# A two-layer transformer kernel on one core: GpSimd applies the layer norms that ScalarE applied, and does the multiply of the softmax normalisation that VectorE did

## The chip, the core and the metric

The kernel is one program on one core of a Trainium2 chip. The core has five instruction streams that matter here: TensorE (PE in the profile, with its weight loads as PEld), VectorE (DVE), ScalarE (ACT), GpSimd (POOL) and SyncE (SP), which issues the DMAs. They run at the same time and wait for one another through semaphores only. The metric is the time of one execution on the device in microseconds (us); lower is better.

## The reference

The input is 2 sequences of 1024 tokens with 128 features, in float32. Four sub-layers follow each other, and after each the result is added to its input and normalised:

```python
x = _layernorm(x + L0_attn(x))   # 16 heads of 8, causal
x = _layernorm(x + L0_ffn(x))    # 8 experts, the best 2 weighted, relu
x = _layernorm(x + L1_attn(x))   # low-rank q and k, 16 heads of 8, causal
x = _layernorm(x + L1_ffn(x))    # an attention of 16 heads of 4, not causal, then 8 experts, gelu

def _layernorm(x, axis=-1, eps=1e-05):
    m = jnp.mean(x, axis=axis, keepdims=True)
    v = jnp.var(x, axis=axis, keepdims=True)
    return (x - m) / jnp.sqrt(v + eps)

def attention(q, k, v):          # per head
    return softmax(scale * q @ k.T, axis=-1) @ v
```

So there are three attentions (two causal, one not) of 32 heads each (16 heads by 2 sequences), and two expert layers. The expert layers compute all 8 experts for all tokens and weight them by a gate.

## The kernel before

**Tiling.** The 2048 tokens are 16 tiles of 128 tokens (`NT`), in 4 chunks of 4 tiles (`NCH`, `TPC`); a sequence is 2 chunks. `x` and `x_plus` hold the tokens on the partitions, 128 features per tile; `xT` holds them turned round, as TensorE needs them.

**Attention.** The heads are numbered g = 0 to 95 and run one after another. Per head TensorE computes the scores twice. First by query (L1332), from which VectorE takes the largest score of each row (`find_max`: L1027 for full blocks, L1023 for blocks at the diagonal, which add the mask `future` first) and then the negated maximum of the head (L1033, `neg_max`). VectorE is two heads ahead (`AHEAD`). GpSimd splits the negated maximum into three bf16 parts (`split_max`, L719 to L726), TensorE turns them (L1354, `max_rows`), ScalarE copies them out (L888), and a DMA puts them among the rows of `qk`. Then TensorE computes the scores by key with the maximum already subtracted (L1346), ScalarE takes the exponential into `probs` (L911), GpSimd clears what lies beyond the diagonal in two chunks of each causal head (`mask`, L752), and TensorE multiplies by the values (L1375) and sums in one PSUM bank for a group of heads.

**Groups.** Heads are in groups of 3, 3, 3, 3, 2, 2 (causal) or 4, 4, 4, 4; that makes 12, 12 and 8 groups in the three attentions. When a group is complete, ScalarE copies the sums (L893), TensorE turns them (L1385), ScalarE copies them to `by_quarter` (L899), GpSimd adds them to `total` (`add_quarters`, L742 to L746, or L737), and VectorE normalises them (`normalise`): a reciprocal of the sum of each row (L1041) and a multiply of all results by it (L1043), which writes `a_tok`. VectorE does this two heads after the group's last head, between two of the head's parts.

**Between the heads.** Everything else (projections, statistics, norms, the next layer's q, k and v, the routing) is cut into steps, and tables filled by `put(...)` name the place at which each is done: `at_head(g, k)`, a part of a head, or `at_unit(f, m, half)`, a half of one of the 32 units (4 chunks by 8 experts) of an expert layer. Each engine goes through the same places in order and does its share of each step, in its function `between`. A step of a place inside the heads is done one place later (`at_place_before`).

**The layer norm** in those steps: VectorE computes mean and variance (`stats`, L1079 and L1082); GpSimd computes `rstd` = 1/sqrt(variance + eps) and `shift` = -mean * rstd (`root`, L676 to L679); ScalarE computes x = x_plus * rstd + shift for the 4 tiles of a chunk (`norm`, L853); TensorE turns the chunk (`xT`, L1422) and ScalarE copies that (L858). Norms are numbered k = 1 to 4, after each of the four sub-layers. The last chunk of k = 4 is VectorE's own (`last_units`), so ScalarE has 15 chunks of norms: 4 each for k = 1, 2, 3, and 3 for k = 4.

**Experts.** Unit by unit TensorE computes the hidden values (L1489), ScalarE applies relu or gelu (L931), TensorE multiplies back (L1501), and VectorE adds the result with its gate to `acc` (L1187). ScalarE does the activation of unit m+1 before the steps of unit m (`experts`, `hid(m + 1)` ahead of `between`).

## Time and profile before

| | us |
|---|---|
| median of 3 runs | 1165.69 (1164.51 to 1167.61) |
| the profiled execution | 1166.3 |
| its span, first to last instruction | 1164.6 |
| TensorE busy | 1077.7 (93%) |
| VectorE busy | 883.9 (76%) |
| ScalarE busy | 764.9 (66%) |
| GpSimd busy | 305.0 (26%) |

The busy times are averages over stages with different limits: the first causal attention runs from about 30 to 280 us, the first expert layer to about 410 us, the second causal attention to about 690 us, the attention without a mask to about 1037 us, and the second expert layer to the end. The mean granted clock of TensorE is 0.987 of full speed. In a list of groups or in a timeline, a row gives the start, the duration, the engine, the line and what is computed; what stands in brackets is how long the engine was idle just before and what ended that.

### The profile page before, as it was taken

The numbers are of one execution on the slowest core, as the hardware profiler recorded it, in microseconds if no ns is written. First come the engines' busy times: TensorE is split into PE (matmuls) and PEld (weight loads), VectorE is DVE, ScalarE is ACT, GpSimd is POOL, SyncE is SP. The second block draws the span as 40 slices with busy tenths as digits, with TensorE's granted clock in tenths as the row PEclk, the third lists the DMA queues.
The fourth block names the chain that finished last, engine by engine and source line by source line (L and its number), as shares of the span: only waits on it lengthen the run. The fifth ranks groups of instructions, "written<-read, shape, count | busy, mean of one in ns | idle before, by whom it ended". The sixth has DMA issues, their size and how long they took to land. (4 is left out here: it accounts for less than half of the span.)

```text
span 1164.6 us, 24392 instructions
## 1 busy us (share of the span) xinstructions
PE 1077.7 (93%) x8338; PEld 569.1 (49%) x8338; DVE 883.9 (76%) x2563; ACT 764.9 (66%) x1527; POOL 305.0 (26%) x843
## 2 busy tenths in 40 slices
PE   8999999989999988999999998898889898899997
PEld 5465665656767655666655532221122221137775
DVE  6999989882433497889978899799999899804435
ACT  4576776766444446777776677888888688875443
POOL 4234433231115225433346211230110100100001
PEclk9899999999999999999999999999999999999999
DMA  7355431100001601344222221002111000000000
GB/s 200 75 121 156 104 84 33 43 23 2 1 1 38 157 22 33 96 106 103 66 75 56 55 38 25 18 18 45 26 36 38 11 18 13 6 1 1 10 10 19
DMA packets 39563, 57.62 MB, mean 49 GB/s; under 512 B 9408, under 2 KB 14992, under 8 KB 39056
## 3 DMA queue, kind: packets, MB, share of 16 engines
q1 hardware_dynamic: 39440, 56.06, 19.6%
q8 instruction: 67, 1.10, 0.4%
q14 instruction: 56, 0.46, 0.1%
HBM read 30.81 MB, written 24.64 MB: 48 GB/s over the span
## 5 line engine op out<-in xcount | busy, mean ns | idle before, releaser
L911 ACT ACTIVATE probs<-bank 128x512 f32<-128x512 f32 x1088 | 575.9, 601 | 214.8 <-PE bank L1346 213.6
L1027 DVE TENSOR_REDUCE tile_max<-bank 128x1 f32<-128x512 f32 x768 | 495.5, 683 | 55.6 <-PE bank L1332 53.2
L1332 PE MATMUL bank<-qk 125*128 125x512 bf16 (+1 forms) x1280 | 387.2, 356 | 54.9 <-DVE tile_max L1027 41.3
L1346 PE MATMUL bank<-qk 128*128 128x128 bf16 (+1 forms) x1664 | 384.6, 309 | 5.9 <-ACT probs L911 5.5
L1375 PE MATMUL bank<-probs,v_head 128*32 128x512 f32 (+3 forms) x3328 | 304.1, 454 | 0.1
L1332 PEld LDWEIGHTS bank<-qk 125*128 125x128 bf16 (+1 forms) x1280 | 105.4, 96 | 333.1 <-DVE tile_max L1027 225.4
L1023 DVE CUSTOM_DVE_ANT_0 bank<-bank,future 128x512 f32<-128x512 f32 (+3 forms) x512 | 243.5, 506 | 22.2 <-PE bank L1332 22.1
L1187 DVE SCALAR_TENSOR_TENSOR acc<-bank,gate,acc 128x128 f32<-128x128 f32 x248 | 69.7, 343 | 158.4 <-PE bank L1501 158.4
L1346 PEld LDWEIGHTS bank<-qk 128*128 128x128 bf16 (+1 forms) x1664 | 138.2, 97 | 68.1 <-ACT probs L911 22.0
L1375 PEld LDWEIGHTS bank<-probs,v_head 128*32 128x32 f32 x3328 | 139.7, 109 | 53.4 <-issue 30.5
L931 ACT ACTIVATE probs<-bank,sb_b 128x512 f32<-128x512 f32 x128 | 81.0, 684 | 123.1 <-PE bank L1489 123.1
L1501 PEld LDWEIGHTS bank<-sb_w,probs 128*128 128x128 f32 x1024 | 123.2, 192 | 23.4 <-issue 22.5
L1501 PE MATMUL bank<-sb_w,probs 128*128 128x128 f32 x1024 | 125.0, 275 | 0.0
L1489 PE MATMUL bank<-xT,sb_w 128*128 128x512 f32 x256 | 121.0, 595 | 0.0
L752 POOL TENSOR_SCALAR_AFFINE_SELECT probs<-probs 128x512 f32<-128x512 f32 x128 | 81.5, 637 | 128.3 <-ACT probs L911 128.3
L719 POOL CAST neg_parts<-neg_max 128x8 bf16<-128x8 f32 x96 | 18.3, 191 | 298.1 <-DVE neg_max L1033 298.1
L1023 DVE DVE_READ_ACCUMULATOR2_ANT tile_max<- 128x1 f32 x512 | 71.9, 140 | 0.0
L1489 PEld LDWEIGHTS bank<-xT,sb_w 128*128 128x128 f32 x256 | 44.1, 191 | 34.0 <-issue 33.4
L742 POOL TENSOR_TENSOR pairs<-by_quarter 128x108 f32<-128x108 f32 (+1 forms) x24 | 9.5, 395 | 114.5 <-ACT by_quarter L899 114.5
L888 ACT ACTIVATE neg_rows<-bank 24x128 bf16<-24x128 bf16 x96 | 24.7, 257 | 15.0 <-PE bank L1354 15.0
L676 POOL TENSOR_SCALAR rstd<-mean_var 128x4 f32<-128x4 f32 (+1 forms) x11 | 2.6, 238 | 121.6 <-DVE mean_var L1082 121.4
L1354 PE MATMUL bank<-ident,neg_parts 128*24 128x128 bf16 x96 | 21.8, 227 | 7.5 <-POOL neg_parts L726 3.2
(148 smaller groups left out, 648.9 us busy)
## 6 DMA issues: line engine op xcount, KB each, us to landing
qk<-qk_parts SPq DMA_DIRECT2D x160, 144.0 KB
qk_parts<-q_parts SPq DMA_DIRECT2D x48, 192.0 KB, 2.4
qk_parts<-k_parts SPq DMA_DIRECT2D x48, 192.0 KB, 2.9
qk_parts<-q_parts SPq DMA_DIRECT2D x24, 96.0 KB, 2.3
qk_parts<-k_parts SPq DMA_DIRECT2D x24, 96.0 KB, 2.9
sb_w<-in_w SPq DMA_DIRECT2D x8, 256.0 KB, 3.7
sb_w<-in_w SPq DMA_DIRECT2D x2, 1024.0 KB, 5.9
qk<-neg_rows SPq DMA_DIRECT2D x96, 6.0 KB
```

The source lines that it names most:

```text
L752: nc.gpsimd.affine_select(out=p, in_=p, compare_op=ALU.is_ge, fill=0.0, base=0, pattern=[[0, 4], [1, P]], channel_multiplier=-1).then_inc( ...
L888: nc.scalar.activation(neg_rows[:, g % RING, :], neg_ps, ACT.Copy).then_inc(sem("neg_rows"), 1)
L911: nc.scalar.activation(probs[:, hd.probs_place(c), :], S2[i % len(S2)][:], ACT.Exp, scale=hd.a.scale).then_inc(sem("probs"), 1)
L931: nc.scalar.activation(hidden[:, m % 2, fb, :], hid_bank(f, m, fb)[:], ACT.Relu if f == 0 else ACT.Gelu, bias=w_sb[f"b1_{f}"][:, FB * e + ...
L1023: ins = nc.vector.tensor_tensor_reduce(out=s1[:, at:at + P * count], in0=s1[:, at:at + P * count], in1=future[:, P * (4 - count):4 * P], s ...
L1027: ins = nc.vector.tensor_reduce(largest, s1[:, at:at + P * count], AX.X, ALU.max)
L1187: ins = nc.vector.scalar_tensor_tensor(acc[:, tile, :], y_bank(f, m)[:, P * t:P * (t + 1)], gate[:, tile, e:e + 1], acc[:, tile, :], ALU.m ...
L1332: ins = mm(s1[:, at:at + P * count], qk[hd.query_rows, hd.place, 0, P * t:P * (t + 1)], qk[hd.query_rows, hd.place, 1, P * k0:P * (k0 + co ...
L1346: ins = mm(s2[:, at:at + P * count], qk[hd.key_rows, hd.place, 1, P * j:P * (j + 1)], qk[hd.key_rows, hd.place, 0, P * q0:P * (q0 + count) ...
L1375: ins = mm(SUM[Q * quarter:Q * (quarter + 1), q:q + P * count], v_head_of(a)[:, hd.v_slot, j, :], probs[:, hd.probs_place(c), at:at + P * ...
L1489: ins = mm(hid_bank(f, m, fb)[:], w_sb[f"w1_{f}"][:, e, P * fb:P * (fb + 1)], xT[:, tokens(c)], start=True, stop=True)
L1501: ins = mm(y[:, P * t:P * (t + 1)], hidden[:, m % 2, fb, P * t:P * (t + 1)], w_sb[f"w2_{f}"][:, e, fb, :], start=fb == 0, stop=fb == FB - 1)
```

## The change

GpSimd takes over two pieces of work. First, all norms with k < 4 (12 chunks of 4 instructions) move from ScalarE (`activation`) to GpSimd (`tensor_scalar` with a multiply and an add). GpSimd does them in the same table's places. Second, `normalise` is split: VectorE keeps the reciprocal (now `inverse`), and GpSimd does the multiply, 32 instructions, in part k = 1 of the head in which VectorE did it, after its own mask of that part. The semaphores are renamed to fit, and VectorE gets a wait ahead of the reciprocal for the multiply of two groups earlier.

```diff
+def by_gpsimd(k, c):
+    return k < 4
...
+        def normed(eng, k, c):
+            by = by_gpsimd(k, c)
+            eng.wait_ge(sem("normed_gpsimd" if by else "normed"), NORMS_OF[by].index((k, c)) + 1)
... GpSimd, between(place)
+                    if kind == "norm" and by_gpsimd(*which):
+                        k, c = which
+                        pool.wait_ge(sem("rstd"), ROOT_OF[(k, c)])
+                        for t in range(TPC * c, TPC * (c + 1)):
+                            ins = nc.gpsimd.tensor_scalar(x[:, t, :], x_plus[:, t, :], rstd[:, t:t + 1], shift[:, t:t + 1],
+                                                          ALU.mult, ALU.add)
+                        ins.then_inc(sem("normed_gpsimd"), 1)
... GpSimd, add_quarters(i)
-                ge(pool, "normalised", 2 * (i - 1))
+                ge(pool, "normalised", i - 1)
... GpSimd
+            def normalise(i):
+                first = GROUPS[i][0]
+                a, G, h = first.a, len(GROUPS[i]), first.h
+                o = total[:, i % 2, :, 0:G * a.dv].rearrange("p t (g d) -> p t g d", g=G)
+                pool.wait_ge(sem("inverse"), i + 1)
+                nc.gpsimd.tensor_tensor(
+                    a_tok[:, of_sequence(first.b), a.hd * h:a.hd * (h + G)].rearrange("p t (g d) -> p t g d", g=G),
+                    o[:, :, :, 1:a.dv], den_inv[:, i % 2, :, 0:G].unsqueeze(3).to_broadcast([P, TB, G, a.hd]),
+                    ALU.mult).then_inc(sem("normalised"), 1)
... GpSimd, head(run, g)
                     if k == 1 and hd.a.causal:
                         mask(g, 1)
+                    if k == 1 and g - 2 >= run.start and HEADS[g - 2].ends_group:
+                        normalise(GROUP[g - 2])
... GpSimd, after the last head of a run
                 add_quarters(GROUP[run.stop - 1])
+                normalise(GROUP[run.stop - 1])
... ScalarE, between(place)
-                    if kind == "norm":
+                    if kind == "norm" and not by_gpsimd(*which):
... VectorE (normalise, now inverse)
                 dve.wait_ge(sem("total"), ADDS[i + 1])
-                nc.vector.reciprocal(den_inv[:, i % 2, :, 0:G], o[:, :, :, 0]).then_inc(sem("normalised"), 1)
-                dve.wait_ge(sem("normalised"), 2 * i + 1)
-                nc.vector.tensor_tensor(
-                    a_tok[:, of_sequence(first.b), a.hd * h:a.hd * (h + G)].rearrange("p t (g d) -> p t g d", g=G),
-                    o[:, :, :, 1:a.dv], den_inv[:, i % 2, :, 0:G].unsqueeze(3).to_broadcast([P, TB, G, a.hd]),
-                    ALU.mult).then_inc(sem("normalised"), 1)
+                ge(dve, "normalised", i - 1)
+                nc.vector.reciprocal(den_inv[:, i % 2, :, 0:G], o[:, :, :, 0]).then_inc(sem("inverse"), 1)
... TensorE, step aT
-                        pe.wait_ge(sem("normalised"), 2 * groups_done)
+                        pe.wait_ge(sem("normalised"), groups_done)
... TensorE, step xT (the store of the output and the step bias wait in the same way)
-                        pe.wait_ge(sem("normed"), NORM_OF[(k, c)])
+                        normed(pe, k, c)
```

The order of VectorE's instructions around the first group's normalisation (head 4 of the first attention), before and then now. `ISA` is the masked maximum (L1023), `TENSOR_REDUCE` the plain one (L1027); in the changed kernel they have the lines 1053 and 1057.

```order
L1027 TENSOR_REDUCE tile_max<-bank 128x1 [waits scores_q]
L1023 ISA bank,tile_max<-bank,future 128x384 [waits scores_q]
L1023 ISA tile_max 128x1
L1023 ISA bank,tile_max<-bank,future 128x128
L1023 ISA tile_max 128x1
L1041 RECIPROCAL den_inv<-total 128x8x3 [waits total]
L1043 TENSOR_TENSOR a_tok<-total,den_inv 128x8x24 [waits normalised]
L1027 TENSOR_REDUCE tile_max<-bank 128x1 [waits scores_q]
L1023 ISA bank,tile_max<-bank,future 128x256 [waits scores_q]
```

Now:

```order
L1057 TENSOR_REDUCE tile_max<-bank 128x1 [waits scores_q]
L1053 ISA bank,tile_max<-bank,future 128x384 [waits scores_q]
L1053 ISA tile_max 128x1
L1053 ISA bank,tile_max<-bank,future 128x128
L1053 ISA tile_max 128x1
L1072 RECIPROCAL den_inv<-total 128x8x3 [waits total]
L1057 TENSOR_REDUCE tile_max<-bank 128x1 [waits scores_q]
L1053 ISA bank,tile_max<-bank,future 128x256 [waits scores_q]
```

The multiply and its wait for the reciprocal have gone from between the maxima; nothing else moved.

GpSimd's instructions in the same head 4, before. The two `AFFINE_SELECT` are the masks, `COPY` is the values of head 6, and the four after the second mask split the maximum of head 6.

```order
L752 AFFINE_SELECT probs<-probs 128x512 [waits probs]
L711 COPY v_head<-v 128x8x9 [waits pv]
L752 AFFINE_SELECT probs<-probs 128x512 [waits probs]
L719 CAST neg_parts<-neg_max 128x8 [waits neg_max,neg_ps]
L721 TENSOR_TENSOR neg_rest<-neg_max,neg_parts 128x8 [waits neg_parts]
L724 CAST neg_parts<-neg_rest 128x8 [waits neg_parts]
L726 TENSOR_TENSOR neg_parts<-neg_rest,neg_parts 128x8 [waits neg_parts]
```

Now:

```order
L779 AFFINE_SELECT probs<-probs 128x512 [waits probs]
L728 COPY v_head<-v 128x8x9 [waits pv]
L779 AFFINE_SELECT probs<-probs 128x512 [waits probs]
L770 TENSOR_TENSOR a_tok<-total,den_inv 128x8x24 [waits inverse]
L736 CAST neg_parts<-neg_max 128x8 [waits neg_max,neg_ps]
L738 TENSOR_TENSOR neg_rest<-neg_max,neg_parts 128x8 [waits neg_parts]
L741 CAST neg_parts<-neg_rest 128x8 [waits neg_parts]
L743 TENSOR_TENSOR neg_parts<-neg_rest,neg_parts 128x8 [waits neg_parts]
```

The multiply stands between the second mask and the split, with a wait for VectorE's reciprocal.

GpSimd's instructions in the first expert layer, from the root of the norm after the attention on, before:

```order
L676 TENSOR_SCALAR rstd<-mean_var 128x8 [waits var]
L677 TENSOR_TENSOR rstd<-rstd,minus_half 128x8 [waits gpsimd_chain]
L678 TENSOR_TENSOR shift<-mean_var,rstd 128x8 [waits gpsimd_chain]
L679 TENSOR_SCALAR shift<-shift 128x8 [waits gpsimd_chain]
L698 TENSOR_TENSOR pick<-pick,small 128x64 [waits route_weights]
L698 TENSOR_TENSOR pick<-pick,small 128x64 [waits gpsimd_chain]
L699 TENSOR_TENSOR gate<-pick 128x64 [waits gpsimd_chain]
```

Now:

```order
L686 TENSOR_SCALAR rstd<-mean_var 128x8 [waits var]
L687 TENSOR_TENSOR rstd<-rstd,minus_half 128x8 [waits gpsimd_chain]
L688 TENSOR_TENSOR shift<-mean_var,rstd 128x8 [waits gpsimd_chain]
L689 TENSOR_SCALAR shift<-shift 128x8 [waits gpsimd_chain]
L695 TENSOR_SCALAR x<-x_plus,rstd,shift 128x128 [waits rstd]
L695 TENSOR_SCALAR x<-x_plus,rstd,shift 128x128 x3
L695 TENSOR_SCALAR x<-x_plus,rstd,shift 128x128 [waits rstd]
L695 TENSOR_SCALAR x<-x_plus,rstd,shift 128x128 x3
L715 TENSOR_TENSOR pick<-pick,small 128x64 [waits route_weights]
L715 TENSOR_TENSOR pick<-pick,small 128x64 [waits gpsimd_chain]
L716 TENSOR_TENSOR gate<-pick 128x64 [waits gpsimd_chain]
```

The eight instructions of the two chunks follow the root directly on GpSimd; in the kernel before they stood on ScalarE, among its activations.

## Rows read from the trace of the kernel before

**Rows 1.** The page, busy time of each engine, its share of the span, and instructions.
```profile
PE 1077.7 (93%) x8338; PEld 569.1 (49%) x8338; DVE 883.9 (76%) x2563; ACT 764.9 (66%) x1527; POOL 305.0 (26%) x843
```

**Rows 2.** Busy us by stretch: PE, PEld, DVE, ACT, POOL; then TensorE's clock, DMA.
```profile
30.00:280.00 250.00, 237.68 (x2250) 143.42 (x2250) 209.66 (x729) 172.04 (x360) 89.01 (x266) 0.98 0.29 75
282.00:410.00 128.00, 123.10 (x713) 89.39 (x712) 52.30 (x219) 54.69 (x99) 33.22 (x50) 1.00 0.20 45
...
815.00:915.00 100.00, 89.02 (x649) 22.74 (x645) 95.47 (x167) 83.00 (x168) 10.33 (x49) 1.00 0.16 31
```

**Rows 3.** TensorE's waits, 30 to 380 us: for whom, us in total, times, longest.
```profile
PE bank L1332 <- DVE tile_max L1023: 4.6, 18, 0.6
...
PE bank L1332 <- DVE tile_max L1027: 3.1, 6, 0.7
```

**Rows 4.** The same, 700 to 1000 us.
```profile
PE bank L1332 <- DVE tile_max L1027: 31.8, 88, 3.7
```

**Rows 5.** Timeline, head 4: VectorE's normalisation, and TensorE after it.
```profile
67.79 0.30 DVE L1041 RECIPROCAL den_inv<-total 128x24 f32<-128x24 f32 x1
68.13 0.36 DVE L1043 TENSOR_TENSOR a_tok<-total,den_inv 128x192 f32<-128x192 f32 x1
68.40 0.68 DVE L1027 TENSOR_REDUCE tile_max<-bank 128x1 f32<-128x512 f32 x1
...
70.01 0.38 PE L1332 MATMUL bank<-qk 125*128 125x512 bf16 x1 [0.26 <-DVE tile_max L1023]
```

**Rows 6.** Timeline, head 7: GpSimd, VectorE and TensorE.
```profile
88.89 1.28 POOL L666 TENSOR_TENSOR x_plus<-x,sb_bo 128x512 f32<-128x512 f32 x1
...
89.35 1.03 DVE L1043 TENSOR_TENSOR a_tok<-total,den_inv 128x192 f32<-128x192 f32 x1
...
91.04 0.39 PE L1332 MATMUL bank<-qk 125*128 125x128 bf16 x2 [0.54 <-DVE tile_max L1027]
```

**Rows 7.** Timeline, third attention: the multiply and what follows it on VectorE.
```profile
831.50 0.29 DVE L1043 TENSOR_TENSOR a_tok<-total,den_inv 128x128 f32<-128x128 f32 x1
831.71 1.88 DVE L1027 TENSOR_REDUCE tile_max<-bank 128x1 f32<-128x512 f32 x3
```

**Rows 8.** Timeline, first expert layer: root, ScalarE's norms, TensorE's transposes.
```profile
304.21 0.26 POOL L679 TENSOR_SCALAR shift<-shift 128x8 f32<-128x8 f32 x1
...
304.92 1.64 ACT L853 ACTIVATE x<-x_plus,shift,rstd 128x128 f32<-128x128 f32 x4
...
306.61 0.66 PE L1422 MATMUL bank<-ident,x 128*128 128x128 f32 x4 [1.10 <-ACT x L853]
...
309.49 0.66 PE L1422 MATMUL bank<-ident,x 128*128 128x128 f32 x4 [0.50 <-ACT x L853]
```

**Rows 9.** Timeline, same layer, the norm after the experts, first chunk.
```profile
339.56 0.25 POOL L679 TENSOR_SCALAR shift<-shift 128x4 f32<-128x4 f32 x1
...
342.77 0.66 PE L1422 MATMUL bank<-ident,x 128*128 128x128 f32 x4 [1.10 <-ACT x L853]
```

**Rows 10.** GpSimd's groups by form: busy us and mean ns of one, then idle.
```profile
L677 POOL TENSOR_TENSOR rstd<-rstd,minus_half 128x8 f32<-128x8 f32 x4 | 6.7, 1676 | 0.3
...
L742 POOL TENSOR_TENSOR pairs<-by_quarter 128x108 f32<-128x108 f32 x16 | 6.7, 419 | 73.3 <-ACT by_quarter L899 73.3
...
L627 POOL TENSOR_SCALAR_AFFINE_SELECT ident<-ident 128x128 f32<-128x128 f32 x1 | 0.3, 294 | 0.2 <-POOL ident L625 0.2
```

**Rows 11.** GpSimd's timeline in head 4: the second mask, then the split.
```profile
69.54 0.64 POOL L752 TENSOR_SCALAR_AFFINE_SELECT probs<-probs 128x512 f32<-128x512 f32 x1 [1.83 <-ACT probs L911]
71.53 0.19 POOL L719 CAST neg_parts<-neg_max 128x8 bf16<-128x8 f32 x1 [1.35 <-DVE neg_max L1033]
```

**Rows 12.** TensorE's timeline after a ScalarE norm: head 22, then head 68.
```profile
204.09 0.39 PE L1346 MATMUL bank<-qk 128*128 128x384 bf16 x2 [0.47 <-ACT probs L911]
...
730.54 0.39 PE L1346 MATMUL bank<-qk 64*128 64x512 bf16 x1 [0.74 <-ACT probs L911]
...
739.35 0.66 PE L1422 MATMUL bank<-ident,x 128*128 128x128 f32 x4 [0.98 <-ACT x L853]
```

More of the change, by code:

```diff
@@ L326 @@
 ROOT_OF = {(step[1], c): i + 1 for i, step in enumerate(ROOTS) for c in step[2]}
-NORM_OF = {step[1:]: i + 1 for i, step in enumerate(NORMS)}
 STATS = [step for place in PLACES for step in BETWEEN[place] if step[0] == "stats"]
@@ L330 @@
 assert all(len([step for step in BETWEEN[place] if step in TAKEN]) <= 1 for place in PLACES)
+def by_gpsimd(k, c):
+    return k < 4
+NORMS_OF = {by: [step[1:] for step in NORMS if by_gpsimd(*step[1:]) == by] for by in (False, True)}
 THIRDS = [step for place in PLACES for step in BETWEEN[place] if step[0] == "split"]
@@ L602, in _ @@
             for c in range(NCH - 1):
-                sp.wait_ge(sem("normed"), NORM_OF[(4, c)])
+                normed(sp, 4, c)
                 store_out(tiles(c))
@@ L664, in between @@
                             loaded(pool, "attn1")
-                            pool.wait_ge(sem("normed"), NORM_OF[(2, c)])
+                            normed(pool, 2, c)
                         nc.gpsimd.tensor_tensor(x_plus[:, tiles(c), :], x[:, tiles(c), :],
@@ L1034, in find_max, with inverse @@
                                             negate=True).then_inc(sem("neg_max"), 1)
-            def normalise(i):
+            def inverse(i):
                 first = GROUPS[i][0]
-                a, G, h = first.a, len(GROUPS[i]), first.h
+                a, G = first.a, len(GROUPS[i])
                 o = total[:, i % 2, :, 0:G * a.dv].rearrange("p t (g d) -> p t g d", g=G)
                 dve.wait_ge(sem("total"), ADDS[i + 1])
-                nc.vector.reciprocal(den_inv[:, i % 2, :, 0:G], o[:, :, :, 0]).then_inc(sem("normalised"), 1)
-                dve.wait_ge(sem("normalised"), 2 * i + 1)
-                nc.vector.tensor_tensor(
-                    a_tok[:, of_sequence(first.b), a.hd * h:a.hd * (h + G)].rearrange("p t (g d) -> p t g d", g=G),
-                    o[:, :, :, 1:a.dv], den_inv[:, i % 2, :, 0:G].unsqueeze(3).to_broadcast([P, TB, G, a.hd]),
-                    ALU.mult).then_inc(sem("normalised"), 1)
+                ge(dve, "normalised", i - 1)
+                nc.vector.reciprocal(den_inv[:, i % 2, :, 0:G], o[:, :, :, 0]).then_inc(sem("inverse"), 1)
             def head(run, g, found):
@@ L1059, in head @@
                     if k == 0 and g - 2 >= run.start and HEADS[g - 2].ends_group:
-                        normalise(GROUP[g - 2])
+                        inverse(GROUP[g - 2])
                 return found
@@ L1191, in experts @@
                     if m == 0:
-                        normalise(last)
+                        inverse(last)
                     between(at_unit(f, m, 1))
```

## The prediction

> **What bounds the kernel now.** I read the page's busy times first [rows 1]. TensorE is busy 93% of the span, GpSimd 26%. The change takes work from VectorE (76%) and ScalarE (66%), so it can gain only where TensorE waits for one of them, or where one of them sets the pace. Busy time by stretch shows where that is [rows 2]. In the first causal attention TensorE is busy 237.7 of 250 us; in the experts 123.1 of 128 us, with VectorE and ScalarE under half busy; in a steady piece of the attention without mask VectorE is busy 95.5 of 100 us and TensorE 89.0. So the first 690 us and the last 120 us go by TensorE plus its waits, and the stretch between goes by VectorE. TensorE's waits by releaser come next: up to 380 us it waits 4.6 + 3.1 = 7.7 us for VectorE's maxima [rows 3], from 700 to 1000 us 31.8 us [rows 4]. Last I read the timeline around each instruction that moves, to see whether one of these waits hangs on it.
>
> **The multiply in the causal attentions (24 of the 32).** It takes VectorE 0.27 us from start to start (68.13 to 68.40), and the reciprocal ahead of it takes 0.34 us because the multiply waits for it [rows 5]; without that wait it should be some 0.07 us less. So about 0.34 us leave VectorE each time. Behind 17 of the 24 multiplies, within 3.5 us, TensorE waits for a maximum that came late, as in [rows 5] at 70.01: 0.26 us. Head by head these waits are 0.26 us in 7 cases, 0.17 or 0.18 us in 5, over 0.34 us in 5. I credit the smaller of wait and 0.34 us: 7 x 0.26 + 5 x 0.174 + 4 x 0.34 = 4.05. The fifth of the last kind is the multiply of 1.03 us beside GpSimd's bias add, 0.96 us from start to start, behind which TensorE waits 0.54 and once more 0.26 us [rows 6]: 0.80. Together 4.85 us. Seven multiplies have no such wait behind them and give nothing. If each freed wait turned up at the next instruction the term would be 0; if the whole 24 x 0.34 came back it would be 8.2. I take 4.8.
>
> **The multiply in the third attention.** Here VectorE sets the pace, so what leaves it leaves the span: 0.21 us from start to start (831.50 to 831.71) [rows 7] and 0.07 for the wait, 0.28 us. Five multiplies lie in the steady part (831 to 1009 us): 1.4 us. Three more (694, 744, 790 us) lie where next-layer projections also load TensorE; all eight would give 2.2. I take 1.4.
>
> **What the multiply costs on GpSimd.** The trace has no such instruction. Two inputs of 108 elements take 0.42 us, of 512 elements 1.28 us, that is 2.1 ns an element [rows 6, 10], so 192 elements take about 0.60 and 128 about 0.46 us: 17 us in all, on an engine with 860 us free. In head 4 VectorE's reciprocal ends at 68.09, GpSimd leaves its second mask at 70.18 and then stands idle 1.35 us until the maximum of head 6 arrives [rows 5, 11]. The multiply fits in that gap, so the split behind it starts when it did. Queued behind it are that split and the next head's mask, for which TensorE waits; only a multiply of more than the gap's 1.35 us would begin to move them. In the third attention the wait for the reciprocal ends three quarters of a head before the split is due. Cost 0.
>
> **The norms in the first expert layer (k = 1 and 2, five chunks).** GpSimd has `shift` at 304.47, but ScalarE first ends the activations of the next unit and starts at 304.92; its four instructions end at 306.56, and TensorE waited 1.10 us, from 305.51. The second chunk costs it 0.50 us more [rows 8]. The chunk of the next norm: `shift` ready at 339.81, TensorE there at 341.67, and again a wait of 1.10 us [rows 9]; two more chunks repeat this (361.15, 397.05, again 1.10 us each, arriving 1.55 and 1.80 us after `shift`). On GpSimd the four follow the root at once. One of them is 128 elements with one tensor input: the nearest row is the select of 128x128, 0.29 us; at the two-input rate it would be 0.46 us; the dearest row per element is the power, 1.68 us for 8 [rows 10], a different algorithm, which I keep as a rival. I take 0.38 us from start to start, 1.55 us for a chunk. Then the first chunk is ready at 306.1 (gain 0.45), the second before TensorE is (0.50), the others at 341.4 (1.10), 0.05 us late (1.05) and in time (1.10): 4.2 us. At 0.46 us an instruction this is 3.5, at 0.29 us 4.7.
>
> GPSIMD Engine Reference of the Trainium skill, § Engine selection, speaks against both moves in one way: it sends elementwise work to VectorE, two-input work being about twice as slow on GpSimd, and calls one-input work roughly line-rate. By it the norms are the cheap half and the multiplies the dear one, which the rows on GpSimd bear out (0.29 against 0.46 us for 128 elements).
>
> **The norms elsewhere.** In the causal attentions TensorE turns the chunk later than GpSimd would have it. The gain is that ScalarE is not held for 1.6 us: 0.47 us behind the norm of head 22 [rows 12], and 0.33 and 0.31 us at 212.1 and 590.0, where TensorE waited for ScalarE's queue: 1.1 us (0 to 1.6). In the third attention the two norms cost TensorE waits of 0.74, 0.70 and 0.98 us (the first and third of them in [rows 12]), 2.4 us; VectorE sets the pace of this attention on the whole, so I let half of it through: 1.2 (0 to 2.4).
>
> **Sum.** 4.8 + 1.4 + 4.2 + 1.1 + 1.2 = 12.7 us. The profiled execution took 1166.3 us (span 1164.6 and 1.7 around it), 0.6 above the median of the runs, so the span should become 1151.9, its execution 1153.6, and the median 1165.7 - 12.7 = **1153.0 us**.
>
> **Rivals.** *Only the norms pay* (1159.2 us): the multiplies' 6.2 us do not come, because TensorE's next limit stands right behind each wait, or because GpSimd's new reads hold up VectorE. For it: TensorE has no time to spare in the causal stretch [rows 2]. Against it: the waits are measured and stand directly behind the multiply. The port is told by [rows 6]: a multiply with two SBUF inputs took 1.03 us, ending just after GpSimd's read, against 0.36 alone [rows 5]. Perfetto Trace Analysis of the Trainium skill, § Optimizing Scalar/DVE Operations, warns that moving work between these two might not help because they share a port; SBUF — State Buffer, § Who interferes with whom, limits this to VectorE instructions with two SBUF inputs or in a two-port mode. By the first page the sum would be 6.5; by the second the multiplies moved are just the ones that collide, and the maxima, with at most one input in SBUF, are safe. The trace has only [rows 6] on this, and agrees.
>
> *Next to nothing* (1163 us): in addition GpSimd's norm instruction costs nearer 0.6 us, so that the first chunk in the experts comes later than ScalarE's and the other three hardly earlier (gain 1.5 us), with 1.1 from ScalarE. The waits of 0.17 to 0.26 us are then model noise.
>
> *Slower* (1190 us): GpSimd's `tensor_scalar` with two operands per partition runs on a slow path. It decides from about 1.1 us an instruction, where the five expert chunks wait 8.5 us longer, as much as the other terms give. At 2 us a chunk takes 8 us: in the experts TensorE waits 5.9, 4.6, 5.1, 5.3 and 5.1 us longer (26), some 2 us at head 22 and 4 where masks and splits are held behind a norm, less 7 for the multiplies: 25 us slower. For it: the power at over 150 ns an element. Against it: the select, a one-input instruction of the same size, at 0.29 us.
>
> **How the numbers follow.** 0.3% (3.5 us) is about what a measurement of this kernel can tell from no change. Forecast 0.62, only the norms 0.18, next to nothing 0.13, slower 0.07. Faster is the first two, 0.80; same 0.13; slower 0.07. The range goes from all upper ends (8.2, 2.2, 4.7, 1.6 and 2.4: 19.1 us, 1147), less a little because all together are unlikely, so 1148, up to just short of the third case, 1162; that leaves out the slower one and most of the third.
>
> **What would show it.** In the new profile: about 0.26 us waits gone behind the 24 reciprocals of the causal attentions; no VectorE instruction of 1.03 us there; TensorE's waits ahead of its transposes of `x` (up to 1.10 us before) down to one or two; the GpSimd norm at 0.3 to 0.45 us an instruction; heads of the third attention at a group's end 0.28 us shorter; GpSimd busy some 35 us more (17 for multiplies, 18 for norms), ScalarE 23 us less. I am wrong if a norm instruction takes over 0.6 us, if TensorE waits for the split maxima in more than the one place it did, or if the maxima themselves grow longer.

## The result, and the profile after

The changed kernel takes 1148.8 us (median of 4 runs, 1146.31 to 1150.53), the kernel before 1165.35 us (4 runs, 1164.51 to 1167.61). The ratio is 0.9853 with a 95% interval of 0.983 to 0.9876: 17.1 us less, and between 14.4 and 19.8. The forecast was 1153.0 us, 12.7 us less. The direction was right and the size was short: 12.7 us where 17.1 were measured. The time lies inside the stated range of 1148 to 1162 us, at its lower edge. The rest of this document looks for the missing 4.4 us.

The profiled execution after took 1146.3 us, its span 1144.6, against 1164.6 before: 20.0 us less. It is the fastest of its four runs, so not all of those 20 us belong to the change.

The page's busy times after, which answer to [rows 1]:

```profile
PE 1067.2 (93%) x8273; PEld 569.3 (50%) x8338; DVE 872.2 (76%) x2531; ACT 745.2 (65%) x1479; POOL 338.2 (30%) x923
```

VectorE has the 32 multiplies less, ScalarE the 48 instructions of the norms, and GpSimd has both (80 more instructions, 33.2 us more). The stretches of [rows 2] (columns as there): the first over the same 250 us, the other two at the places where the same work now lies.

```profile
30.00:280.00 250.00, 238.88 (x2240) 147.28 (x2273) 204.63 (x715) 171.92 (x357) 98.01 (x288) 0.98 0.28 75
277.00:401.00 124.00, 122.83 (x713) 89.36 (x712) 51.80 (x218) 47.22 (x79) 42.22 (x71) 1.00 0.20 46
785.00:885.00 100.00, 88.99 (x647) 20.99 (x643) 97.19 (x167) 84.09 (x171) 10.98 (x53) 1.00 0.19 36
```

The expert stretch holds the same 713 TensorE matmuls in 124 us instead of 128. TensorE's waits up to 380 us (for whom, us in total, times, longest), which answer to [rows 3]:

```profile
PE bank L1358 <- DVE tile_max L1053: 3.6, 12, 0.6
...
PE bank L1358 <- DVE tile_max L1057: 1.1, 3, 0.5
PE bank L1448 <- POOL x L695: 1.1, 2, 0.9
```

The waits for maxima fell from 7.7 to 4.7 us. From 700 to 1000 us, though, they did not fall at all against [rows 4] (31.8 us in 88):

```profile
PE bank L1358 <- DVE tile_max L1057: 32.1, 91, 3.7
```

In that attention TensorE waits for VectorE all along, 91 times in 300 us. What a saving is worth there can't be read from the sum of the waits, only from how far apart the heads lie.

Head 4 shows the exchange, first on VectorE, then on GpSimd, then on TensorE (they answer to [rows 5] and [rows 11]):

```profile
67.60 0.30 DVE L1072 RECIPROCAL den_inv<-total 128x24 f32<-128x24 f32 x1
67.81 0.63 DVE L1057 TENSOR_REDUCE tile_max<-bank 128x1 f32<-128x512 f32 x1
```

```profile
69.35 0.63 POOL L779 TENSOR_SCALAR_AFFINE_SELECT probs<-probs 128x512 f32<-128x512 f32 x1 [1.84 <-ACT probs L941]
69.95 0.52 POOL L770 TENSOR_TENSOR a_tok<-total,den_inv 128x192 f32<-128x192 f32 x1
71.00 0.19 POOL L736 CAST neg_parts<-neg_max 128x8 bf16<-128x8 f32 x1 [0.53 <-DVE neg_max L1063]
```

```profile
69.48 0.38 PE L1358 MATMUL bank<-qk 125*128 125x512 bf16 x1
```

From the reciprocal to the next maximum VectorE now needs 0.21 us instead of 0.61. The multiply fills GpSimd's gap, and the split behind it still waits for VectorE. TensorE's wait of 0.26 us is gone.

**The ledger.** In every head TensorE turns the split maxima once (L1354 before, L1380 after): 96 markers, which are the same instruction in every variant. I compare their starts between two traces. A step is what the distance of two neighbouring markers shrank by; it bears the number of the later one. At most heads it repeats to 0.02 us from kernel to kernel. The exceptions are heads 1, 2 and 12 (head 12 takes 6.89 to 7.80 us in the thirteen traces, whatever the kernel) and the heads in which TensorE's granted clock was at half for a stretch. Around head 9, before and after:

```profile
88.44 0.23 PE L1354 MATMUL bank<-ident,neg_parts 128*24 128x128 bf16 x1
...
96.26 0.23 PE L1354 MATMUL bank<-ident,neg_parts 128*24 128x128 bf16 x1
```

```profile
87.91 0.23 PE L1380 MATMUL bank<-ident,neg_parts 128*24 128x128 bf16 x1
...
94.73 0.23 PE L1380 MATMUL bank<-ident,neg_parts 128*24 128x128 bf16 x1
```

96.26 - 88.44 = 7.82 us before and 94.73 - 87.91 = 6.82 after: a step of 1.00 us, behind the multiply that took 1.03 us [rows 6]. All steps, sorted by cause (the experiments below bear the sorting out), against the forecast:

| term | forecast, us | steps found | us |
|---|---|---|---|
| multiply, causal attentions | 4.8 | 15 heads, 0.21 to 0.46 each, once 1.00 | 5.6 |
| multiply, third attention | 1.4 | 9 heads, 0.37 to 0.39 each | 3.4 |
| norms, first expert layer | 4.2 | one, over the whole layer | 3.9 |
| norms, causal attentions | 1.1 | 0.80, 0.75, 0.79 | 2.3 |
| norms, third attention | 1.2 | 2.58 within the 4.16 of head 70 | 2.6 |
| sum | 12.7 | | 17.8 |
| TensorE's clock, heads 70 and 88 | - | 1.58 within the same 4.16, and 0.31 | 1.9 |
| head 12, no cause assigned | - | 0.17 | 0.2 |

With 0.2 us at the start this accounts for the 20.0 us between the two spans, to 0.1 us. The causes give 17.8, within the interval of the ratio.

Head 88, from marker 87 to marker 88, holds neither a multiply nor a norm. TensorE's clock is the last column but two (0.50 is the lower of its two levels, 1.2 GHz, 1.00 the upper, 2.4 GHz). Before, then after:

```profile
926.60:933.40 6.80, 6.62 (x27) 1.18 (x31) 5.17 (x11) 3.72 (x8) 1.80 (x8) 0.50 0.00 1
```

```profile
907.40:914.20 6.80, 5.98 (x26) 0.98 (x29) 5.18 (x11) 3.09 (x6) 1.79 (x8) 0.50 0.00 0
```

Marker 87 stands at 932.72 before and at 914.15 after, so before head 88 has 0.7 us of the half clock in it and after none. It takes 10.51 us before and 10.21 after. In the other traces it takes 10.20 or 10.21 us where the stretch is over by its start, and 10.63, 10.83 and 11.11 where 0.9, 1.3 and 1.9 us of it reach in (the experiments below with the norms alone, the split root and two norms).

### The profile page after: what moved, and what is told of

It is laid out like the page before. It is cut to its first block and busy times, and to the rows that moved or that the text cites. A ratio compares the mean times of both kernels' runs of the same rounds, so it can differ in the third digit from the quotient of the medians.

```text
span 1144.6 us, 24357 instructions
## 1 busy us (share of the span) xinstructions
PE 1067.2 (93%) x8273; PEld 569.3 (50%) x8338; DVE 872.2 (76%) x2531; ACT 745.2 (65%) x1479; POOL 338.2 (30%) x923
## 3 DMA queue, kind: packets, MB, share of 16 engines
q1 hardware_dynamic: 39440, 56.06, 19.8%
## 5 line engine op out<-in xcount | busy, mean ns | idle before, releaser
L1372 PE MATMUL bank<-qk 128*128 128x128 bf16 (+4 forms) x1599 | 360.0, 306 | 3.9 <-ACT probs L941 3.6
L1372 PEld LDWEIGHTS bank<-qk 128*128 128x128 bf16 (+1 forms) x1664 | 138.6, 97 | 64.0 <-ACT probs L941 17.6
L1380 PE MATMUL bank<-ident,neg_parts 128*24 128x128 bf16 x96 | 21.8, 227 | 7.3 <-POOL neg_parts L743 3.2
```

Of the source, the lines that this page charges most:

```text
L1372: ins = mm(s2[:, at:at + P * count], qk[hd.key_rows, hd.place, 1, P * j:P * (j + 1)], qk[hd.key_rows, hd.place, 0, P * q0:P * (q0 + count) ...
```

## The experiments

**The multiply alone.** The changed kernel with all norms back on ScalarE:

```diff
 def by_gpsimd(k, c):
-    return k < 4
+    return False
```

> The changed kernel with all norms back on ScalarE: only the multiply is on GpSimd. Theory (the two halves are independent, each returns the waits that hang on it): the step between the traces at the group ends of the causal attentions is 5.8 us in all and of the third attention 3.7 us, so 9.5 us less than before, 1156 us, with no change in the expert layers. Rival 'only the norms pay' from the prediction: within 2 us of before. Rival 'overlap' (the norms had freed the same waits already): clearly more than 9.5 us, 12 or above.

**The norms alone.** The kernel before, in which VectorE keeps the multiply, with the norms of the change:

```diff
+def by_gpsimd(k, c):
+    return k < 4
... GpSimd, between(place)
+                    if kind == "norm" and by_gpsimd(*which):
... ScalarE, between(place)
-                    if kind == "norm":
+                    if kind == "norm" and not by_gpsimd(*which):
```

> The kernel before with only the 12 norm chunks moved to GpSimd; VectorE keeps its multiply. Theory (independent halves): 3.9 us in the first expert layer, 2.3 in the causal attentions and 4.2 in the third attention, 10.4 us in all, 1155 us. The prediction's own terms for this half: 6.5 us, 1159 us. Overlap: the sum of the two halves is then well off 20 us of the profiled executions.

On that chip the kernel before took 1166.07 us (16 runs). The multiply alone: 1156.82 us (1153.3 to 1157.65), ratio 0.9913 [0.9891, 0.9935], 10.1 us less. The norms alone: 1157.2 us (1153.79 to 1157.98), ratio 0.9905 [0.9878, 0.9932], 11.1 us less. By the ledger they are 5.6 + 3.4 = 9.0 and 3.9 + 2.3 + 2.6 = 8.8 us. Both halves pay and they add up within their intervals (10.1, from 7.6 to 12.7, and 11.1, from 7.9 to 14.2). *Only the norms pay* forecast nothing from the multiplies, and falls. The steps of the multiply in the table stand in the first of these traces with the same values, to 0.01 us, save head 87, where the half-clock stretch is 3.4 us long and not 6.8; they are missing in the second. For the norms it is the other way round (0.95 us and not 0.79 at head 55). That is what sorts the table. Head 12, which I had counted with the multiply in the 5.8 that I expected, shrinks by 0.38 us with the norms alone too, and the 3.7 had head 88 in it. The 4.2 us that I expected of the third attention's norms were the whole step of head 70, clock included.

**Two chunks of norms alone.** The kernel before, with only the two norms of the third attention on GpSimd:

```diff
+def by_gpsimd(k, c):
+    return k == 3 and c >= 2
```

> The kernel before with only two norm chunks moved (k = 3, the two chunks of the second sequence, which fall into the third attention). Theory: there ScalarE is loaded so highly that a norm of 1.6 us between two exponentials stops TensorE and then VectorE, and nothing catches up: 4.2 us less, 1161 us. Rival (the prediction's term, VectorE sets the pace and hides half): 1.2 us less.

1163.55 us over 10 runs, against 1166.07 over 16 runs of the kernel before on that chip; ratio 0.9973 [0.9961, 0.9986], so 3.1 us (1.6 to 4.5) by the ratio and 2.5 by the medians. That excludes the 1.2 of the prediction's term, but not my 4.2. The step at head 70 is again 4.16 us, of which the ledger gives 2.58 to the norms, a little more than TensorE's three waits of 0.74, 0.70 and 0.98 us [rows 12]. So all of the waits came back, not the half I let through. In this trace TensorE turns both chunks without waiting, here the first:

```profile
733.56 0.66 PE L1439 MATMUL bank<-ident,x 128*128 128x128 f32 x4
```

With the norms on ScalarE the three waits stand as before (the trace of the multiply alone):

```profile
722.74 0.39 PE L1372 MATMUL bank<-qk 64*128 64x512 bf16 x1 [0.73 <-ACT probs L941]
723.83 0.39 PE L1372 MATMUL bank<-qk 64*128 64x512 bf16 x1 [0.70 <-ACT probs L941]
729.97 0.66 PE L1448 MATMUL bank<-ident,x 128*128 128x128 f32 x4 [0.98 <-ACT x L883]
```

VectorE's rows of the same place say why they count in full. First the multiply alone, then the changed kernel:

```profile
726.15 2.49 DVE L1057 TENSOR_REDUCE tile_max<-bank 128x1 f32<-128x512 f32 x4 [2.08 <-PE bank L1358]
...
730.99 0.69 DVE L1057 TENSOR_REDUCE tile_max<-bank 128x1 f32<-128x512 f32 x1 [0.89 <-PE bank L1358]
```

```profile
720.09 2.48 DVE L1057 TENSOR_REDUCE tile_max<-bank 128x1 f32<-128x512 f32 x4 [0.71 <-PE bank L1358]
722.75 1.89 DVE L1057 TENSOR_REDUCE tile_max<-bank 128x1 f32<-128x512 f32 x3 [0.17 <-PE bank L1358]
```

VectorE itself stood idle here, waiting for TensorE, and for less time once the norms had left ScalarE. It does not set the pace in this part of the attention, whatever its busy share is on the whole.

**The multiply without its stall.** The kernel before; VectorE keeps the multiply but does one maximum between the reciprocal and it.

```diff
                 nc.vector.reciprocal(den_inv[:, i % 2, :, 0:G], o[:, :, :, 0]).then_inc(sem("normalised"), 1)
+            def multiply(i):
...
                 dve.wait_ge(sem("normalised"), 2 * i + 1)
... head
                         for i in range(found, upto):
                             find_max(i)
+                            if left:
+                                multiply(left.pop())
...
                         normalise(GROUP[g - 2])
+                        left.append(GROUP[g - 2])
...
```

> The kernel before, all work on its old engine, but VectorE does one maximum between the reciprocal and the multiply that waits for it. That takes away the stall (0.34 to 0.22 us from start to start in the causal attentions, 0.38 to 0.26 in the third) and no work. Theory (every bit of VectorE's time at these places counts): 0.12 us at each of 8 places of the third attention and at 17 causal ones, 3.0 us less in the profiled execution. Rival (the stall is hidden, only the multiply's own time counts): no change.

1162.91 us (7 runs), ratio 0.9964 [0.9948, 0.998]: 4.2 us less (2.3 to 6.1). VectorE's rows in head 4, where the spacing from reciprocal to maximum was 0.34 us ahead of the multiply [rows 5] and is now 0.22:

```profile
69.87 0.30 DVE L1041 RECIPROCAL den_inv<-total 128x24 f32<-128x24 f32 x1
70.09 0.63 DVE L1027 TENSOR_REDUCE tile_max<-bank 128x1 f32<-128x512 f32 x1
70.63 0.34 DVE L1048 TENSOR_TENSOR a_tok<-total,den_inv 128x192 f32<-128x192 f32 x1
70.89 0.42 DVE L1023 CUSTOM_DVE_ANT_0 bank<-bank,future 128x256 f32<-128x256 f32 x1
```

So the same work without the wait gives 0.18 or 0.19 us back at 21 groups' ends, in all three attentions, and 0.60 at head 9, where the multiply meets less of the bias add (it took 0.60 us). Of the 0.19, 0.12 is the wait; the rest is that the maximum behind the reciprocal takes 0.63 us and not 0.68. The prediction had put the wait at 0.07 us, which was too low. Where the prediction had found no late maximum for TensorE behind a causal group's multiply, the whole change returned nothing, as it had said.

**The collision at 89 us.** The kernel before, with the second bias add placed one head earlier:

```diff
-for c, g in enumerate((4, 6, 8, 10)):
+for c, g in enumerate((4, 5, 8, 10)):
```

> The kernel before with one GpSimd instruction moved: the bias add of the second chunk (128x512, 1.28 us) stands a head earlier, so that it no longer overlaps VectorE's multiply of head 7, which took 1.03 us beside it. Theory (the multiply was held by GpSimd's read): it takes 0.36 us like the others, and TensorE reaches the turn of the maxima of head 9 about 0.66 us earlier, measured from head 6 (the step of 1.00 us of the changed kernel there, less the 0.34 us of an ordinary group). Rival (the 1.03 us had another cause, a wait for something else in head 7): it stays at 1.03 us, no step.

One run: 1166.99 us, where the kernel before ran between 1164.64 and 1168.8 on that chip, so the total tells nothing. The rows do. The multiply that took 1.03 us [rows 6]:

```profile
89.17 0.36 DVE L1043 TENSOR_TENSOR a_tok<-total,den_inv 128x192 f32<-128x192 f32 x1
89.45 0.68 DVE L1027 TENSOR_REDUCE tile_max<-bank 128x1 f32<-128x512 f32 x1
```

0.36 us instead of 1.03, with GpSimd idle beside it, and a step of 0.67 us at head 9. The same was seen at two more places: beside a GpSimd instruction with two inputs the multiply took 0.65 us at 607.3 before, and 1.16 us at 459.9 in the kernel without the stall. The rule of the Trainium skill weighed in the prediction (SBUF — State Buffer, § Who interferes with whom) holds in this case. The maxima, which by that page are safe, did not lengthen beside GpSimd's new work either: after, 24 whole ones that overlap a multiply or a norm there took 0.68 us each at the median, and so did the 471 with GpSimd idle.

**How much slack a norm on GpSimd has.** The changed kernel; each norm instruction is done twice, once into a tile that nobody reads (ahead of it, cut here, stand that tile and a wait for the norm of the same chunk before):

```diff
...
-                            ins = nc.gpsimd.tensor_scalar(x[:, t, :], x_plus[:, t, :], rstd[:, t:t + 1], shift[:, t:t + 1],
-                                                          ALU.mult, ALU.add)
+                            for into in (spare, x):
+                                ins = nc.gpsimd.tensor_scalar(into[:, t, :], x_plus[:, t, :], rstd[:, t:t + 1],
+                                                              shift[:, t:t + 1], ALU.mult, ALU.add)
```

> The changed kernel with each of GpSimd's 48 norm instructions done twice (once into a spare tile), so a chunk takes 3.4 us in place of 1.7. Theory (GpSimd has room everywhere but in the first expert layer, where TensorE waits for the norm directly): TensorE's waits ahead of its transposes of x grow by 1.5, 0.9, 1.5, 1.8 and 1.6 us in the expert layer, 7.3 us in all, and under 1 us is added in the attentions. Rival (GpSimd's order matters in the attentions too: masks and split maxima are held up): 2 us or more are added between the turns of the maxima of heads 22 to 25, 53 to 55 and 67 to 70.

One run: 1163.9 us, span 1162.2, so 17.6 us longer than after. TensorE's waits from 280 to 412 us, in this kernel and in the changed one:

```profile
PE bank L1452 <- POOL x L699: 8.0, 4, 2.6
```

```profile
PE bank L1448 <- POOL x L695: 1.1, 2, 0.9
```

The waits in the expert layer grew by 6.9 us, as expected (7.3), though the layer grew by 10.2. In this trace it holds two stretches of half clock, from 306.9 and 364.9 us, which the trace after has not; they begin 0.4 and 1.3 us behind waits of 2.58 and 1.96 us, so they may well be part of the price. In the attentions I had expected under 1 us and found 5.4, at heads 25, 35, 55 and 70. That is the amount of the rival (2 us or more), by another path. Beside each stands a wait of TensorE of 0.7 to 1.8 us ahead of a transpose of `x`, the longest here:

```profile
595.39 0.66 PE L1452 MATMUL bank<-ident,x 128*128 128x128 f32 x4 [1.79 <-POOL x L699]
```

So the norms in the attentions have less slack on GpSimd than one chunk's time, 1.74 us, and in these heads no wait of TensorE for a mask or a split was added.

**The last layer's norms too.** The changed kernel with three more chunks on GpSimd:

```diff
-    return k < 4
+    return True
```

> The changed kernel with the three norm chunks of k = 4 on GpSimd as well. In the second expert layer nothing turns the result, only the store waits for it, and ScalarE is under half busy. Theory (a norm costs only where TensorE waits for it or for ScalarE behind it): the same as the changed kernel, within 0.5 us. Rival (ScalarE's 1.6 us delay the next activation there): 1 to 3 us less.

1148.13 us (4 runs, 1146.3 to 1151.98), ratio 0.9839 [0.981, 0.9869]: the same as the changed kernel.

**Is the third attention VectorE's?** The prediction said that it sets the pace there. If so, work moved off its way, or added to it, must show in every head. The changed kernel with `neg_max` taken only behind the next head's first maximum:

```diff
                 ins.then_inc(sem("max_taken"), 1)
+                take_neg_max()
                 if c == a.chunks - 1:
...
-                    nc.vector.tensor_reduce(neg_max[:, hd.slot, :], tile_max[:, hd.slot], AX.X, ALU.max,
-                                            negate=True).then_inc(sem("neg_max"), 1)
+                    ready.append(g)
...
```

> The changed kernel, with one more stall taken from VectorE: the negated maximum of a head is computed after the first maximum of the next head instead of directly behind the last maximum that it waits for. That saves about 0.11 us a head and moves no work to another engine. Theory (in the third attention VectorE sets the pace, all of what leaves it comes back; in the causal ones only where TensorE waits): 0.11 us at each of some 30 heads, 3.3 us less than the changed kernel in the third attention, and 1 to 3 us in the causal ones; 1144 us. Rival (the maximum then comes 0.5 us later to GpSimd, and TensorE, which took its split 0.4 to 0.6 us after it was ready, waits for it): no gain or a loss.

1149.4 us (1146.62 to 1151.44), ratio 0.9852 [0.9831, 0.9873]: no gain, which is the rival's outcome. The expected 3.3 us did not come; from the marker of head 64 to that of head 95 the trace is 0.95 us longer than after. Six heads in which a group is normalised are 0.08 to 0.11 us shorter, twelve others, from 66 to 94, are 0.09 to 0.10 longer, and head 84 is 0.35 longer. Then the reverse: the changed kernel with a `memset` of 128x128 on VectorE in each of the 32 heads, once in the middle of the head, once right behind `neg_max`.

```diff
+                if not a.causal and c == 2:
+                    nc.vector.memset(extra[:, g % 16, :], 0.0)
```

```diff
                     nc.vector.tensor_reduce(neg_max[:, hd.slot, :], tile_max[:, hd.slot], AX.X, ALU.max,
                                             negate=True).then_inc(sem("neg_max"), 1)
+                    if not a.causal:
+                        nc.vector.memset(extra[:, g % 16, :], 0.0)
```

> The changed kernel with one idle VectorE instruction added per head of the third attention (a memset of 128x128 in a spare tile, 32 in all), behind the third maximum of the head, where VectorE runs without waiting. New theory (VectorE sets the pace inside a head, TensorE at the change of heads, where VectorE waits about 0.18 us for the first scores): the memset's start-to-start time, estimated at 0.1 to 0.2 us from VectorE's other short instructions, comes on top of the span 32 times: 3 to 6 us between the turns of the maxima of heads 63 and 95. Old theory (VectorE sets the pace throughout): the same.

> The same memset, but directly behind the negated maximum of each head, at the change of heads. New theory: it fills the time in which VectorE waits for TensorE's scores there, so less than 1 us is added in the same stretch. Old theory (VectorE sets the pace throughout): the same 3 to 6 us as with the memset inside the head.

One run each: 1151.01 and 1148.67 us, which by themselves tell nothing at this size. The instruction costs VectorE 0.08 us from start to start:

```profile
822.06 0.17 DVE L1067 MEMSET extra<- 128x128 f32 x1
822.14 1.32 DVE L1058 TENSOR_REDUCE tile_max<-bank 128x1 f32<-128x512 f32 x2
```

If VectorE set the pace everywhere, 32 times 0.08 us = 2.6 us would show. In the middle it shows as 0.08 or 0.09 us at seven heads (71, 75, 79, 83, 87, 91, 95) and as nothing in the others; these seven are where a group ends and the reciprocal stands. That is 0.6 us, so both theories, with their 3 to 6 us, were wrong there. Behind `neg_max` it shows at eleven other heads (66, 68, 74, 76, 78, 80, 82, 86, 90, 92, 94), 0.9 us in all, as expected. Head 88 has a half-clock stretch in it and tells nothing. So whether VectorE's time counts depends on the place within the head: in its middle it counts only in the one head in four that has the normalisation, at its end in about one of three, and at the other places VectorE has at least 0.08 us to spare. What sets the pace there I have not found.

**An earlier start in the experts.** The changed kernel, the last norms on GpSimd too, and a root for each chunk, the first of them one place earlier:

```diff
-    put(at[4], ("stats", k, c1))
-    put(at[5], ("root", k, (c0, c1)))
+    put(at[4], ("stats", k, c1), ("root", k, (c0,)))
+    put(at[5], ("root", k, (c1,)))
...
-    return k < 4
+    return True
```

> The changed kernel with all norms but the last chunk's on GpSimd, and the root of the two chunks after an attention computed chunk by chunk, the first one place earlier. In the first expert layer the changed kernel's TensorE still waits 0.85 us for the first chunk's norm, behind a power of 1.68 us for 8 columns; with 4 columns the power takes 1.04 us, so the chunk is ready some 0.6 us earlier. Theory: the step in the first expert layer is 0.6 us, nothing elsewhere; the time cannot be told from the changed kernel's. Rival (the additional 2 us of GpSimd's work hold up masks and split maxima in the attentions): 0.5 us or more is lost at heads 21 to 24 and 52 to 55.

1149.85 us (4 runs, 1149.0 to 1150.76), ratio 0.986 [0.9839, 0.9881]: no gain, and the first expert layer is 0.14 us longer, not 0.6 shorter. The second chunk's root now stands in GpSimd's queue ahead of the first chunk's norm and costs what the split saved. GpSimd, then TensorE:

```profile
300.16 0.24 POOL L689 TENSOR_SCALAR shift<-shift 128x4 f32<-128x4 f32 x1
300.48 0.23 POOL L686 TENSOR_SCALAR rstd<-mean_var 128x4 f32<-128x4 f32 x1
300.79 1.05 POOL L687 TENSOR_TENSOR rstd<-rstd,minus_half 128x4 f32<-128x4 f32 x1
...
302.43 2.62 POOL L695 TENSOR_SCALAR x<-x_plus,rstd,shift 128x128 f32<-128x128 f32 x6
```

```profile
304.23 0.66 PE L1448 MATMUL bank<-ident,x 128*128 128x128 f32 x4 [0.95 <-POOL x L695]
```

None of the variants is clearly faster than the changed kernel.

## Why the prediction came out as it did

**The multiply, causal attentions: 4.8 forecast, 5.6 measured.** The mechanism was right and the term too small. I had credited the smaller of TensorE's wait and 0.34 us. The seven heads with waits of 0.26 us returned 0.33, four of the five with 0.17 or 0.18 returned 0.22 and the fifth nothing, and three with more returned 0.45. What left VectorE ahead of the next maximum was 0.39 us (0.61 to 0.22), since the wait for its own reciprocal costs 0.12 us and not 0.07. The collision was as read: 1.00 us at head 9 (forecast 0.80), of which 0.67 is shown by moving the bias add.

**The multiply, third attention: 1.4 forecast, 3.4 measured; the largest error.** Two factors. From the reciprocal to the second maximum behind it VectorE took 1.19 us before and 0.81 after, so 0.38 us left it and not 0.28; and it came back at eight groups' ends, not at five. Those where projections also load TensorE, which I had left out, paid like the rest. A ninth step, 0.37 us at head 90, is in every trace with the multiply on GpSimd and in no other; that head has no multiply, and why it gained is open. The reason that I gave, that what leaves VectorE leaves the span there, held for the heads with the normalisation. It is no rule for the others, as the moved `neg_max` and the two added instructions show: there it depends on the place.

**The multiply on GpSimd: 0 forecast, 0 found.** One took 519 ns for 192 elements (0.60 expected), and nothing was held up. GpSimd's own waits for the reciprocal, 17.3 us in all, show in no wait of another engine, and TensorE waits for the split maxima once, 3.2 us, as before:

```profile
L770 POOL TENSOR_TENSOR a_tok<-total,den_inv 128x192 f32<-128x192 f32 (+1 forms) x32 | 14.9, 466 | 17.3 <-DVE den_inv L1072 17.3
```

**The norms in the experts: 4.2 forecast, 3.9 measured.** The price of one instruction was set between 0.29 and 0.46 us at 0.38; it is 448 ns long and 0.43 from start to start, a chunk 1.74 us:

```profile
L695 POOL TENSOR_SCALAR x<-x_plus,rstd,shift 128x128 f32<-128x128 f32 x48 | 20.8, 448 | 0.4
```

At the two-input end, 0.46 us, the forecast was 3.5. TensorE's two later arrivals, which I gave as 1.55 and 1.80 us behind `shift`, are 1.65 and 1.87 us in the trace before; that changes the sum by 0.05 us. The first chunk still makes TensorE wait 0.85 us (1.10 before [rows 8]), and the chunk of [rows 9] is in time:

```profile
299.32 0.26 POOL L689 TENSOR_SCALAR shift<-shift 128x8 f32<-128x8 f32 x1
...
301.47 0.66 PE L1448 MATMUL bank<-ident,x 128*128 128x128 f32 x4 [0.85 <-POOL x L695]
...
333.77 0.24 POOL L689 TENSOR_SCALAR shift<-shift 128x4 f32<-128x4 f32 x1
334.12 1.74 POOL L695 TENSOR_SCALAR x<-x_plus,rstd,shift 128x128 f32<-128x128 f32 x4
...
335.92 0.66 PE L1448 MATMUL bank<-ident,x 128*128 128x128 f32 x4
```

The price is one and a half times the select's, so what the prediction drew from the Trainium skill (GPSIMD Engine Reference, § Engine selection), that one-input work is the cheap kind on GpSimd, did not hold here: one norm lasts 0.45 us and a two-input multiply of 128 elements 0.41 us.

**The norms, causal: 1.1 forecast, 2.3 measured.** The three places were the right ones, but each gave 0.75 to 0.80 us where I had credited 0.31 to 0.47, the wait shown. The failed step is this cap: the 1.6 us that left ScalarE were worth more than the one wait that carried ScalarE's name. Where the rest of each lay I have not traced.

**The norms, third attention: 1.2 forecast, 2.6 measured.** Halving them for the attention's overall bound was the failed step. The waits fell where VectorE itself waited for TensorE.

**What no term of the sum had: the clock.** The trace before holds, in the same head 70, a stretch in which TensorE's granted clock was at half. Just ahead of it TensorE was busy 5.71 of 7.90 us and had two waits for ScalarE's exponentials, of 0.74 and 0.70 us. Before it and in it, the columns as in [rows 2]:

```profile
724.00:731.90 7.90, 5.71 (x41) 1.26 (x37) 7.71 (x14) 7.06 (x16) 0.94 (x5) 1.00 0.00 1
732.00:735.40 3.40, 3.40 (x17) 0.99 (x16) 0.00 (x0) 1.46 (x4) 0.54 (x1) 0.50 0.56 108
```

and the same work with the multiply alone, whose clock did not fall behind the same two waits:

```profile
716.00:733.00 17.00, 13.84 (x99) 3.85 (x95) 13.46 (x24) 15.26 (x34) 2.23 (x11) 1.00 0.11 22
```

Without the stretch the step between before and the multiply alone is still 1.58 us at this head, where neither a multiply nor a norm differs; VectorE's idle time there fell from 3.63 to 2.08 us. I read that as the stretch's price. The same difference stands at head 38, which takes 8.34 us before with such a stretch and 6.82 in the multiply alone without. Whether the 1.6 us belong to chance or to the change is open. Of the four traces in which ScalarE does these two norms, three have a half-clock stretch at head 70 (before, the stall taken away, the bias add apart); of the nine in which GpSimd does them, none has. That speaks for a share of the norms' move in it, and no run tests it by itself. In the timed runs the whole change is worth 17.1 us, with either reading inside its interval.

**The rivals.** *Next to nothing* rested on a norm instruction near 0.6 us and on waits that were model noise: the instruction took 0.43, and the waits came back more than whole. *Slower* needed 1.1 us. Doubling the instruction, to some 0.87 us of work, cost 17.6 us of span in its one run, nearly all of the gain. So the case was unlikely, but its turning point lies nearer 0.9 us than 1.1, an estimate from that run.

**Why the time still fell inside the range.** Three of the five terms came out above their own upper ends: 3.4 us against 2.2 for the multiply in the third attention, 2.3 against 1.6 and 2.6 against 2.4 for the norms in the attentions. The range held, by 0.8 us, because its largest allowance, 8.2 us for the multiply in the causal attentions, was used to 5.6 only. That is luck in the range, and not a sign that each term was known so well.

## What to carry to other kernels

A wait is credited where it stands, by who is idle there: the bound of a whole stage, used as a discount on it, was wrong by half. When work leaves an engine, count its whole start-to-start cost, the wait on the engine's own last result included. Where the consumer waited behind it, 15 of 16 places in the causal attentions returned more than was credited for the wait; where it did not wait, nothing came back. An idle engine's price per instruction is worth measuring, but so is its slack: the same norms at twice the time would have given the gain back.

## What the runs showed that was not expected

- TensorE's granted clock falls to half for stretches of about 3.4 or 6.8 us between heads 3 and 95. Head 87 has one in all thirteen traces, head 38 in ten, the others come and go. Most begin near a wait of TensorE of 0.7 us or more (3.67 us in head 87, 3.2 us ahead of head 38), but those at heads 63 to 65, in four traces, and one at head 86 have only waits of up to 0.33 us ahead of them. One of 3.4 us cost 1.0 to 1.6 us of span. In the trace without the stall they cost 1.1, 1.0 and 1.05 us at heads 38, 69 and 86; with a start that was 2.1 us later they hid its gain of some 4.6 us, and its span was 1164.7 against 1164.6 before. What sets them off I can't say.
- On VectorE the reciprocal takes 0.34 us from start to start with an instruction behind it that waits for its semaphore, and 0.22 without: 0.12 us for that wait.
- A GpSimd norm instruction of 128x128 with two operands per partition costs 0.43 us, half again the select's 0.29.
